# Key and value units first in the setup of a two-layer kernel, its loads in another order

## The reference, cut to what matters

```python
def _layernorm(x, eps=1e-05):                      # per token, over 256
    return (x - mean(x)) / sqrt(var(x) + eps)
Q = _layernorm(x) @ Wq      # 2048 x 256 by 256 x 128
K = ctx @ Wk                # 1601 x 256 by 256 x 128
V = ctx @ Wv                # 1601 x 256 by 256 x 128
attn = softmax(Q @ K.T / sqrt(128))
out = (attn @ V) @ Wo + bo + _layernorm(x)
out = out @ Wfc             # then a layer norm, a residual sum, routed and shared experts, and the second layer
```

## Time and profile before

| | |
|---|---|
| median of 3 executions | 1089.59 us (1089.4 to 1092.72) |
| the profiled execution, its own time | 1086.07 us |
| its span | 1084.0 us |
| TensorE busy in the span | 1002.7 us (92%) |
| VectorE, ACT, POOL busy | 678.4, 511.8, 403.2 us |
| TensorE's granted clock, mean | 0.965 of full speed |
| the setup, to the last VectorE instruction of its block | 45.34 us |
| first instruction of TensorE | 10.98 us |

### The profile page before, as it was taken

One profiled execution on the slowest core, in us unless ns is written; L12 is line 12 of the kernel. 1 busy time (PEld: TensorE's weight loads), 2 busy tenths in 40 slices (PEclk: granted clock), 3 DMA queues, 4 the chain that ended last, 5 costly groups with the idle time before them and its releaser, 6 DMA issues. The chain is left out here.

```text
span 1084.0 us, 18715 instructions
## 1 busy us (share of the span) xinstructions
PE 1002.7 (92%) x6840; PEld 921.6 (85%) x6840; DVE 678.4 (63%) x1605; ACT 511.8 (47%) x1041; POOL 403.2 (37%) x636
## 2 busy tenths in 40 slices
PE   5999999499899999997899999999999999999983
PEld 4899998388899999985787799989898999999983
DVE  5577776359487888763476455454445677766652
ACT  4446665323277777751345433333334444444431
POOL 5324445507124443317411100000015767677530
PEclk9999999699999999999799999999999999999985
DMA  7200000101188788855103400000001101111000
GB/s 221 79 1 2 1 2 1 57 22 59 53 250 248 249 262 255 249 151 153 56 8 98 108 1 12 9 1 1 2 1 21 25 21 31 25 31 30 11 10 11
DMA packets 56881, 76.54 MB, mean 71 GB/s; under 512 B 5536, under 2 KB 37408, under 8 KB 56800
## 3 DMA queue, kind: packets, MB, share of 16 engines
q1 hardware_dynamic: 38896, 50.04, 15.4%
q0 software_dynamic: 15648, 22.81, 7.2%
q10 hardware_dynamic: 2256, 2.62, 0.7%
HBM read 61.43 MB, written 14.02 MB: 70 GB/s over the span
## 5 line engine op out<-in xcount | busy, mean ns | idle before, releaser
L43 PE MATMUL bank<-V_hi,XT_lo 128*128 128x256 f32 x416 | 123.8, 298 | 1.2 <-DVE XT_lo L2220 1.2
L2220 DVE TENSOR_TENSOR XT_lo<-bank,XT_lo 128x512 fp32r<-128x512 f32 x116 | 73.3, 633 | 77.5 <-ACT XT_lo L1913 77.2
L1913 ACT ACTIVATE XT_lo<-bank 128x512 fp32r<-128x512 f32 x116 | 63.8, 552 | 119.4 <-PE bank L1672 118.8
L45 PE MATMUL bank<-V_hi,XT_lo 128*128 128x256 f32 x416 | 117.3, 282 | 0.0
L44 PE MATMUL bank<-V_lo,XT_lo 128*128 128x256 f32 x416 | 117.1, 282 | 0.0
L443 DVE TENSOR_TENSOR expert_w_lo<-sraw,expert_w_hi 128x1024 fp32r<-128x1024 f32 x72 | 88.2, 1224 | 33.1 <-ACT expert_w_hi L439 30.3
L2225 DVE TENSOR_REDUCE part<-wide 128x1 f32<-128x402 f32 (+1 forms) x116 | 72.4, 624 | 38.6 <-PE wide L45 36.6
L43 PE MATMUL wide<-expert_w_hi,XT_hi 128*128 128x402 f32 (+1 forms) x232 | 91.4, 394 | 3.4 <-issue 2.4
L45 PE MATMUL wide<-expert_w_hi,XT_hi 128*128 128x402 f32 (+1 forms) x232 | 85.5, 369 | 0.0
L44 PE MATMUL wide<-expert_w_lo,XT_hi 128*128 128x402 f32 (+1 forms) x232 | 85.5, 368 | 0.0
L43 PEld LDWEIGHTS bank<-V_hi,XT_lo 128*128 128x128 f32 x416 | 78.6, 189 | 4.6 <-DVE XT_lo L2220 2.9
(11 more groups left out here) (454 smaller groups left out, 3248.6 us busy)
## 6 DMA issues: line engine op xcount, KB each, us to landing
sraw<-w1T SPq DMA_DIRECT2D x25, 512.0 KB, 5.7
sraw<-w3T SPq DMA_DIRECT2D x25, 512.0 KB, 6.6
sraw<-w2T SPq DMA_DIRECT2D x25, 512.0 KB, 7.6
XT_hi<-queries POOLq DMA_DIRECT2D x16, 256.0 KB, 3.2
routed_results<-rys POOLq DMA_DIRECT2D x15, 256.0 KB
X<-x ACTq DMA_DIRECT2D x4, 512.0 KB, 7.8
token_rows<-Fx SPq DMA_DIRECT2D x4, 512.0 KB, 4.9
out<-X SPq DMA_DIRECT2D x16, 128.0 KB, 1.7
```

The source lines that it names most:

```text
L43: pe.matmul(out, wh, xh, start=first, stop=False)
L45: return pe.matmul(out, wl, xh, start=False, stop=last)
L1913: act.activation(weights(g, nk, 0), transposed(g, nk), ACT.Copy).then_inc(sem["high"], 1)
L2220: dve.tensor_tensor(weights(g, nk, 1), transposed(g, nk), weights(g, nk, 0).bitcast(F32), ALU.subtract).then_inc(sem["low"], 1)
```

## The change

Keys and values of a part now come before its queries, and the first unit is keys 0, so TensorE's first work needs no tokens. The loads follow: SP issues Wk and Wv (`lda`, now two), context 0, Wq (`ldq`, new), tokens 1, context 1, tokens 2, then as before with tokens 3 between contexts 2 and 3. Only tokens 0 stay on ACT's queue. The first weights are split in two pieces, Wk with Wv and then Wq. `context_low(0)` moves from POOL to VectorE (`ctx_low0`, new), and the lists of ACT, VectorE and TensorE are written anew: VectorE's normalise(1) stands before token_low(0), its statistics(2) before low(1), its normalise(2) before low(2) and statistics(3), its normalise(3) before token_low(2); ACT's `second_weights` moves ahead of token_high(2).

```diff
-                UNITS = [(kind, b) for b in range(3) for kind in "qkv"] + [("f", 0)] + [(kind, 3) for kind in "qkv"]
+                UNITS = [(kind, b) for b in range(3) for kind in "kvq"] + [("f", 0)] + [(kind, 3) for kind in "kvq"]
...
+                def context_low(eng, b):
+                    x = ctx_cols(b)
+                    eng.wait_ge(ctx_high, b + 1)
+                    eng.tensor_tensor(CT_lo[:, :, x], ctf[:, :, x], CT_hi[:, :, x].bitcast(F32), ALU.subtract)\
+                       .then_inc(ctx_low if b else ctx_low0, 1)
...
+                    def tokens(g):
+                        sp.dma_start(X[:, g * 4 * D:(g + 1) * 4 * D].rearrange("p (i d) -> p i d", d=D),
+                                     A["x"][0, g * 512:(g + 1) * 512, :].rearrange("(i p) d -> p i d", p=P)).then_inc(ldx[g], 16)
-                    weight("L0_xattn_Wq", lda)
                     weight("L0_xattn_Wk", lda)
                     weight("L0_xattn_Wv", lda)
                     context(0)
+                    weight("L0_xattn_Wq", ldq)
+                    tokens(1)
                     context(1)
+                    tokens(2)
                     weight("L0_xattn_WoT", ldb)
                     weight("L0_xattn_Wfc", ldb)
                     weight("L0_ffn_router_wT", ldb)
                     context(2)
+                    tokens(3)
                     context(3)
...
                 def _(act):
-                    for g in range(4):
-                        act.dma_start(X[:, g * 4 * D:(g + 1) * 4 * D].rearrange("p (i d) -> p i d", d=D),
-                                      A["x"][0, g * 512:(g + 1) * 512, :].rearrange("(i p) d -> p i d", p=P)).then_inc(ldx[g], 16)
+                    act.dma_start(X[:, 0:4 * D].rearrange("p (i d) -> p i d", d=D),
+                                  A["x"][0, 0:512, :].rearrange("(i p) d -> p i d", p=P)).then_inc(ldx[0], 16)
...
-                    act.wait_ge(lda, 16 * 3)
-                    act.activation(Wb_hi[:, 0:na], raw[:, 0:na], ACT.Copy).then_inc(first_high, 1)
+                    act.wait_ge(lda, 16 * 2)
+                    act.activation(Wb_hi[:, nq:na], raw[:, nq:na], ACT.Copy).then_inc(first_high, 1)
+                    context_high(0)
                     normalise(0)
-                    context_high(0)
+                    act.wait_ge(ldq, 16)
+                    act.activation(Wb_hi[:, 0:nq], raw[:, 0:nq], ACT.Copy).then_inc(first_high, 1)
+                    context_high(1)
+                    high(0)
                     token_high(0)
                     normalise(1)
-                    context_high(1)
-                    high(0)
+                    high(1)
                     token_high(1)
+                    high(2)
+                    context_high(2)
                     normalise(2)
-                    high(1)
-                    context_high(2)
-                    high(2)
+                    high(3)
+                    high(4)
+                    second_weights()
                     token_high(2)
                     normalise(3)
                     context_high(3)
-                    high(3)
-                    high(4)
-                    token_high(3)
-                    second_weights()
                     high(5)
                     act.wait_ge(ldf, 32)
                     act.activation(fold_hi[:, :], fold_raw[:, :], ACT.Copy).then_inc(fold_high, 1)
-                    for u in range(6, 10):
+                    high(6)
+                    token_high(3)
+                    for u in range(7, 10):
                         high(u)
...
                     inverse(0)
                     inverse(1)
-                    context_low(0)
+                    context_low(pool, 1)
                     inverse(2)
-                    context_low(1)
+                    context_low(pool, 2)
                     inverse(3)
-                    context_low(2)
-                    context_low(3)
+                    context_low(pool, 3)
...
                     statistics(0)
+                    first_weights(0, slice(nq, na))
+                    context_low(dve, 0)
                     statistics(1)
-                    dve.wait_ge(first_high, 1)
-                    dve.tensor_tensor(Wb_lo[:, 0:na], raw[:, 0:na], Wb_hi[:, 0:na].bitcast(F32), ALU.subtract).then_inc(first_low, 1)
                     normalise(0)
+                    first_weights(1, slice(0, nq))
+                    low(0)
+                    normalise(1)
+                    token_low(0)
                     statistics(2)
-                    token_low(0)
-                    normalise(1)
-                    statistics(3)
-                    low(0)
+                    low(1)
                     token_low(1)
                     normalise(2)
-                    low(1)
                     low(2)
-                    token_low(2)
-                    normalise(3)
+                    statistics(3)
                     low(3)
                     low(4)
+                    normalise(3)
+                    token_low(2)
+                    second_weights()
+                    low(5)
+                    low(6)
                     token_low(3)
...
+                    pe.wait_ge(first_low, 1)
+                    unit(0)
                     pe.wait_ge(ident_known, 1)
                     turn(0)
-                    pe.wait_ge(first_low, 1)
-                    unit(0)
+                    unit(1)
                     turn(1)
-                    unit(1)
+                    pe.wait_ge(first_low, 2)
                     unit(2)
                     unit(3)
+                    unit(4)
                     turn(2)
-                    unit(4)
                     unit(5)
+                    unit(6)
                     turn(3)
-                    for u in range(6, 10):
+                    for u in range(7, 10):
                         unit(u)
                     fold()
```

More of the change, by code:

```diff
@@ L2498, in build @@
                 xn = sb(ctx, "xn0", [P, 2, 4 * D])
-                (lda, ldb, ldv, ldf, ldo, made, ident_known, half_known, padded, bo_spread) = sems(
-                    ctx, "lda ldb ldv ldf ldo made ident_known half_known padded bo_spread")
+                (lda, ldq, ldb, ldv, ldf, ldo, made, ident_known, half_known, padded, bo_spread) = sems(
+                    ctx, "lda ldq ldb ldv ldf ldo made ident_known half_known padded bo_spread")
                 ldx = sems(ctx, "ldx0 ldx1 ldx2 ldx3")
                 ldc = sems(ctx, "ldc0 ldc1 ldc2 ldc3")
-                (first_high, first_low, second_high, second_low, ctx_high, ctx_low, fold_high, fold_low, folded, fold_kept,
-                 fold_stored) = sems(ctx, "first_high first_low second_high second_low ctx_high ctx_low fold_high fold_low "
+                (first_high, first_low, second_high, second_low, ctx_high, ctx_low0, ctx_low, fold_high, fold_low, folded, fold_kept,
+                 fold_stored) = sems(ctx, "first_high first_low second_high second_low ctx_high ctx_low0 ctx_low fold_high fold_low "
                                           "folded fold_kept fold_stored")
@@ L2510, in build @@
                 na = spec0["L0_xattn_WoT"][0]
-                UNITS = [(kind, b) for b in range(3) for kind in "qkv"] + [("f", 0)] + [(kind, 3) for kind in "qkv"]
+                nq = spec0["L0_xattn_Wk"][0]
+                UNITS = [(kind, b) for b in range(3) for kind in "kvq"] + [("f", 0)] + [(kind, 3) for kind in "kvq"]
                 turning = [(wide[:, 0:512], wide[:, 512:1024]), (wide[:, 1024:1536], wide[:, 1536:2048])]
@@ L2714, in low, with first_weights, second_weights @@
                         dve.tensor_tensor(lo, src, hi.bitcast(F32), ALU.subtract).then_inc(unit_low, 1)
+                    def first_weights(k, x):
+                        dve.wait_ge(first_high, k + 1)
+                        dve.tensor_tensor(Wb_lo[:, x], raw[:, x], Wb_hi[:, x].bitcast(F32), ALU.subtract).then_inc(first_low, 1)
+                    def second_weights():
+                        dve.wait_ge(second_high, 1)
+                        dve.tensor_tensor(Wb_lo[:, na:nw + 2 * P], raw[:, na:nw + 2 * P], Wb_hi[:, na:nw + 2 * P].bitcast(F32),
+                                          ALU.subtract).then_inc(second_low, 1)
                     statistics(0)
+                    first_weights(0, slice(nq, na))
+                    context_low(dve, 0)
                     statistics(1)
-                    dve.wait_ge(first_high, 1)
-                    dve.tensor_tensor(Wb_lo[:, 0:na], raw[:, 0:na], Wb_hi[:, 0:na].bitcast(F32), ALU.subtract).then_inc(first_low, 1)
                     normalise(0)
+                    first_weights(1, slice(0, nq))
+                    low(0)
+                    normalise(1)
+                    token_low(0)
                     statistics(2)
-                    token_low(0)
-                    normalise(1)
-                    statistics(3)
-                    low(0)
```

(17 more changed lines are left out.)

4 lines of the change are left out of this document (removed).

## The result

The changed kernel took 1083.46 us in the median (1081.55 to 1084.38, 6 runs) beside 1089.9 us for the kernel before (1088.76 to 1092.72, 6 runs): ratio 0.9936 with a 95% interval of 0.9924 to 0.9948, so 5.7 to 8.3 us faster. The profiled execution took 1081.55 us with a span of 1079.5, where 1081.4 and 1079.3 were forecast from the profile of before. In the pair of profiled executions the gain is 4.5 us, and in the setup itself 3.7 us: the first matmul of the first attention starts at 42.06 in place of 45.78. The experiments had to settle two things: which steps made the 3.7, and where the rest of the gain in time comes from.

The account below looks back on a forecast made before the run. TensorE's row of work after a late start bounds the setup: 9.7 start + 27.0 work + 1.8 slow clock + 0.8 gaps = 39.3, block end 40.6; gain 4.7 gives 1084.9 us, range 1082.0 to 1088.8.

Parts of the forecast that it names:

- The loads by byte count: Setup loads: landings from bytes at 354 GB/s after 5 us plus 1.0 us; context 0 at 7.4, tokens 1 at 9.3.
- Rival (a): Setup loads: tokens 1 land late, at 11, delaying turn(0); gain 3.2 us; chance 0.17 together with Rival (e).
- rival (d): Setup loads: tokens 1 land at 15.0 or later, making the kernel slower, 1093.7 us at 18; chance 0.05.
- Rival (e): Setup start: context 0 lands at 8.7 or later, no start before 10.9; gain 3.4; chance 0.17 together with Rival (a).
- The start of TensorE: Setup: keys 0 starts at 9.7 us, after VectorE's low half of context 0, 1.3 before anything started before.
- Queries 0: Setup: its first matmul waits 0.1 to 0.3 us for token_low(0), ending at 17.3, and starts at 17.4.
- The slow clock: TensorE's first setup work: pace doubles 3.7 to 5 us after work begins, costing 1.8 us against 2.9 before.
- The account of before: Old setup on TensorE: 10.98 start + 27.0 work + 3.85 idle + 2.9 slow clock = 44.7 us.
- Rival (b): Setup: the clock rises only at 18 because idle pieces fall between keys 0 and turn(0); gain 2.8; chance 0.08.
- the lighter price of 0.4: VectorE's normalise(1) beside POOL's context_low(1): the smaller delay considered; 2.1 us was taken; the lighter ends the setup 0.3 earlier.
- The gap ahead of turn(3): Setup: TensorE waits 0.7 us for ACT's normalise(3), queued behind second_weights; the 1.39 before the fold goes.
- rival (c): After 46 us: later low-clock stages shift the gain by 1 to 2 us either way; chance 0.15, both sides.

Follow-up runs that it names:

- r6: Changed kernel with tokens 1 to 3 issued by ACT's queue again: 1085.06 us, ratio 0.9968 to the kernel before.
- r1: The changed kernel run again without edits: 1072.8 us, ratio 0.9963 to the kernel before.
- r3: Changed kernel with queries 3 before keys and values 3, VectorE's normalise(1) before low(0), second_weights behind context_high(3): 1071.75 us, ratio 0.996 to the kernel before.
- r7: Changed kernel with VectorE's normalise(1) ahead of low(0): 1080.2 us, ratio 0.9927 to the kernel before.
- r8: Changed kernel with ACT's second_weights moved behind normalise(3) and context_high(3): 1081.59 us, ratio 0.9938 to the kernel before.
- r9: The changed kernel run a third time without edits: 1071.76 us, ratio 0.9947 to the kernel before.
- r12: Changed kernel with queries 3 first of the last three units: 1071.99 us, ratio 0.9938 to the kernel before.
- r4_warm: Changed kernel with 44 unused transposes of the identity ahead of keys 0 on TensorE: 1070.71 us, ratio 0.9944 to the kernel before.

## Why the prediction was right, and where its sizes were off

The time lies inside the range, 1.4 us below the number forecast, and in the setup the forecast's case is the one that happened: an earlier start on the context, two idle times gone, a new one of 0.7 ahead of turn(3). That the profiled time came within 0.2 us of the forecast is luck: the setup gave 1.0 less than the 4.7, and the later stages of that pair gave 0.7 more. Point by point:

**The loads by byte count** held within 0.4 us: tokens 0 at 5.80 (5.39 forecast, the row of before), the first weights 6.16 (6.0), context 0 7.57 (7.4), tokens 1 9.4 (9.3). Rival (a), tokens 1 late behind the backlog, needed 11 and rival (d) 15; neither came near. Rival (e), context 0 at 8.7 or later, is what r6 shows (9.1) when the tokens stay in a second queue. So the loads' order in one queue is a condition of the gain, and the forecast had worked it out as bytes at 354 GB/s.

**The start of TensorE**: 10.03, 9.7 forecast. This is the first mis-sized term, 0.33: context 0 landed 0.17 late, and from the end of the low half (9.89) to the matmul it took 0.14, which the forecast had put at nothing. In the six later executions with this front of the list and no transposes ahead (r1, r3, r7, r8, r9, r12) it was 9.46 to 9.76.

**Queries 0** is the second mis-sized place: 18.19, 17.4 forecast. TensorE's own row was late by the clock: turn(0) took 1.56 to the next matmul (1.3 forecast) and values 0 2.88 (2.7), 0.45 together, so that with the late start turn(1) begins at 17.17 and not at 16.4. But that isn't what set queries 0. They wait for token_low(0), which ended at 18.04 (17.3 forecast) and whose chain holds neither values 0 nor turn(1). POOL's context_low(1) began at 14.05 and not at 13.4, because inverse(1) started at 11.70 and took 2.35, where the forecast's places (11.5 and 13.4) leave 1.9, and VectorE's normalisation waited it out. With the clock as forecast turn(1) would have been through at about 17.5, and queries 0 would still have started behind 18.04.

**The slow clock** itself: the forecast had the rise 3.7 to 5 us behind the first matmul; the six profiles of the two kernels show 3.3 to 6.1. Its price for the kernel before was reckoned from the row of turn(0), 1.94, against 0.79; the 1.94 holds the end of the last transpose, and from start to start eight slow ones take 1.56. The account of before adds up even so, since its idle time is counted from the end of that row. Hence the gain in the setup is 3.7 in one pair and 5.4 in two, on either side of 4.7, mostly by what the kernel before loses. Rival (b), a clock that rises at 18, happened in no run of this list; the latest rise was at 15.6 (r8).

**The pieces behind that** are right in kind: the normalisation pair beside POOL took 2.70, with 0.7 + 2.1 forecast. The Trainium skill (SBUF — State Buffer, "Who interferes with whom") has two such instructions exclude each other for the whole length; this normalisation has one tensor as input, so the page has it not by the rule on two SBUF inputs that the prediction names but among the operations that can take both of VectorE's ports. 2.70 beside POOL and 0.74 ahead of it in r7 agree, and the lighter price of 0.4 is refuted for this pair. The gap ahead of turn(3) is 0.69 (0.7 forecast), behind ACT's split of the second weights as worked out; the fold waits no more. What was missed there: POOL's context_low(3) took 1.64 where 0.81 stood in the earlier trace rows, beside VectorE's subtraction at 28.30, hidden. From turn(1) to the last matmul another 0.35 gathers in tenths. The tail is 1.36 (1.3 forecast), and the fold's store ended at 40.9 (39.9), hidden.

So the block ends at 41.74 and not at 40.6: 0.8 up to queries 0 (0.2 of it the late start, the rest mostly POOL's inverse(1) in the chain to token_low(0)) and 0.35 in small pieces. The seam to the next stage was 0.1 shorter than before, and 3.7 of the 4.7 are there.

**From 42 us to the end** the forecast said that nothing changes, and gave 0.15 to rival (c), that a later stage gives or takes 1 to 2 us. Single executions do this (the table of places), in both directions and for the kernel before as much; as an effect of the change it is not shown. (Of the three stages that it names, the trace of before has the last fall to the lower clock from about 1043 on and not at 1030.) The 7.0 us of the first comparison lie above what the repeats give (about 4.0 and 5.7, each by its ratio), and the intervals overlap (5.7 to 8.3, 2.2 to 5.8, 3.6 to 7.8). Whether the first six runs were on a chip that gains more or only on the good side of the spread stays open; no run settles it.

**What the forecast would have done better with**: it costed the second weights' new place as a wait that could be had back, and so did I in r8 and r3. The wait sits on ACT's whole list from 24.7 to 31, and to move one item in it moves the wait from turn(3) to the fold.

## What to carry to other kernels

Where a phase starts with nothing but loads, put them in one queue in the order of need and count bytes at the rate that the trace shows: here this gave each landing within 0.4 us, and a second queue with later data cost the first operand 1.6. When a gap is closed by moving work on another engine, look which wait is second in line on that engine before it is called a gain: 0.69 at turn(3) and 0.74 at the fold were the same overload of ACT. And an engine that begins at the slow clock pays at its own start: take the slow stretch from several executions, since one profile of the kernel before was 1.4 us from the next. Last, an engine that gets faster only gains up to its next wait: with the clock up from the start, 0.5 of some 2 us arrived until the normalisation beside POOL was moved as well.

## What the runs showed of the hardware that was not expected

- The pace of TensorE in the setup is slow for a time that differs between executions of the same list of instructions: 3.3, 5.4 and 6.1 us behind unit 0's first matmul in the kernel before, 4.6, 5.6 and 3.6 behind keys 0's in the kernel after (matmuls of 512 columns 0.43 apart, then 0.23).
- Transposes of the identity alone bring it up: in r4_warm 7 a us at 3 to 4 us, 11 a us at 8 to 9, with the first at 1.58. The matmuls behind them start fast.
- The granted clock stands at 1.00 in both of these windows, and in 0 to 41 us as a whole. In this stretch the pace has to be read from the spacing of the matmuls and not from that column, unlike in the experts' stage, where it showed 0.50.
- Two normalisations on VectorE of 0.74 us are held to 2.70 by one subtraction of POOL that began 0.16 us earlier (kernel after); begun 0.5 ahead of it, they lose nothing (r7_norm_first).
